# Four-layer graph network kernel: the one-hot matrices of the edge build get sixteen slots, four result buffers and a chunk-major stationary

## What is computed

```python
h = max(layernorm(x), 0); x = x + L0(h)   # sum of neighbours, two-layer MLP, layernorm
h = max(layernorm(x), 0); x = x + L1(h)   # 8-head attention over the edges, then an MLP
h = max(layernorm(x), 0); x = x + L2(h)   # softmax of the edge weights, both directions
h = max(layernorm(x), 0); x = x + L3(h)   # mean over neighbours, two linear maps
```

## Time and profile before

| | us |
|---|---|
| median of 3 runs (range) | 1474.82 (1468.77 to 1477.15) |
| the profiled execution | 1477.18 |
| its span, first to last instruction | 1475.4 |
| PE busy over the span | 1281.1 (87%) |
| DVE busy | 652.5 (44%) |
| ACT busy | 425.2 (29%) |
| set-up, to the first `hot` of DVE | about 49 |
| window stage, first matmul to first of line 424 | 50.05 to 365.04 |

### The profile page before, as it was taken

The page is one execution under the profiler, slowest core; times in us unless marked ns, Lnnn a source line. Parts: engine busy times, 40 slices in busy tenths (PEclk is TensorE's granted clock), DMA queues, the critical chain, the costliest instruction groups (busy, mean ns, idle before and its releaser), DMA issues.

```text
span 1475.4 us, 18831 instructions
## 1 busy us (share of the span) xinstructions
PE 1281.1 (87%) x6205; PEld 753.9 (51%) x6205; DVE 652.5 (44%) x1702; ACT 425.2 (29%) x728; POOL 126.7 (9%) x95
## 2 busy tenths in 40 slices
PE   1577777777999965998999999999998998899998
PEld 0244444444555432455777777775436555445543
DVE  6666666664401723103656565655565202430022
ACT  2401122222002422202555555553334202431000
POOL 0000000000445122100000000000233000100000
PEclk9878879778999987999999999999999999769999
DMA  4012344445777200000000000006000050000001
GB/s 131 0 34 58 99 136 124 137 123 143 280 262 267 86 0 28 30 28 1 1 2 1 1 1 1 2 2 233 1 0 30 0 202 1 1 29 0 0 29 41
DMA packets 41610, 93.86 MB, mean 64 GB/s; under 512 B 5113, under 2 KB 9920, under 8 KB 41526
## 3 DMA queue, kind: packets, MB, share of 16 engines
q1 hardware_dynamic: 41526, 92.74, 19.7%
HBM read 51.76 MB, written 34.56 MB: 59 GB/s over the span
## 4 chain that ended last, share of the span: by engine, by line
PE 78%; DVE 8%; issue 6%; ACT 4%; DVEq 2%; DMA 1%; SPq 0%; POOLq 0%; POOL 0%; ACTq 0%
PE PS L390 13%; PE PS L466 7%; PE PS L598 7%; PE PS L584 6%; PE PS L424 6%; PE PS L711 6%; PE PS L559 6%; PE PS L744 5%; PE PS L530 5%; PE PS L682 3%; PE PS L690 3%; PE PS L520 3%; PE PS L439 2%; DVE HT L865 2%; PE PS L463 2%
## 5 line engine op out<-in xcount | busy, mean ns | idle before, releaser
L390 PE MATMUL PS<-HT,R 125*128 (+1 forms) x988 | 243.3, 379 | 96.5 <-DVE HT L865 42.8
L865 DVE TENSOR_SCALAR HT<-BC,K 125x626 f16 (+1 forms) x494 | 193.0, 443 | 117.5 <-PE PS L390 71.6
L390 PEld LDWEIGHTS PS<-HT,R 125*128 x988 | 138.4, 158 | 201.4 <-issue 179.6
L960 DVE CUSTOM_DVE_ANT_0 HT<-PS,CD 128x1250 f32<-128x1250 f32 (+1 forms) x80 | 116.4, 1455 | 71.8 <-issue 71.8
L584 PE MATMUL PS<-K,HT 128*128 128x128 f32 (+2 forms) x800 | 120.4, 281 | 9.6 <-ACT R L1203 9.6
L1126 ACT COPY HT<-PS 128x626 f32<-128x626 f32 x80 | 54.6, 683 | 254.7 <-PE PS L390 254.7
L598 PE MATMUL PS<-R 128*64 128x128 f32 (+2 forms) x1600 | 113.0, 278 | 0.3
L1209 ACT ACTIVATE HT<-HT,soft 128x1250 f32<-128x1250 f32 (+1 forms) x80 | 106.3, 1333 | 11.7 <-DVE soft L963 11.6
L584 PEld LDWEIGHTS PS<-K,HT 128*128 128x128 f32 (+2 forms) x800 | 82.9, 140 | 43.7 <-issue 23.8
L559 PE MATMUL PS<-R 64*128 64x512 f32 (+3 forms) x480 | 96.5, 534 | 4.8 <-DVE soft L960 3.1
L1203 ACT COPY R<-PS 128x512 f32<-128x512 f32 (+1 forms) x120 | 65.2, 578 | 112.6 <-PE PS L584 112.6
(11 more groups left out here) (182 smaller groups left out, 1416.9 us busy)
## 6 DMA issues: line engine op xcount, KB each, us to landing
edge_parts<-HT SPq DMA_DIRECT2D x80, 234.4 KB
X<-edge_parts SPq DMA_DIRECT2D x15, 625.0 KB, 5.3
R<-edge_parts SPq DMA_DIRECT2D x15, 625.0 KB, 5.4
CD<-HT SPq DMA_DIRECT2D x160, 39.1 KB
edge_counts<-CD SPq DMA_DIRECT2D x10, 625.0 KB, 5.8
CD<-edge_sums SPq DMA_DIRECT2D x1, 6250.0 KB, 21.2
CD<-edge_counts SPq DMA_DIRECT2D x1, 6250.0 KB, 18.9
X<-in_x SPq DMA_DIRECT2D x2, 2304.0 KB
```

Source lines behind the costliest of these rows:

```text
L390: i = mm(bank(b0 + h, PIECE), stat, hot[:, h * PIECE:(h + 1) * PIECE], start=first, stop=True, skip_group_check=True)
L865: return ve.tensor_scalar(slot, iota[0:EC, :], K1[0:EC, K_BASE + w:K_BASE + w + 1], col, ALU.add, ALU.is_equal)
L960: ve.tensor_tensor_reduce(Pb[s][a][0:n], PS[0:n, a * N:(a + 1) * N], cd[0:n, t, :], 1.0, -3e38, ALU.add, ALU.max, soft[0:n, s, a:a + 1]).t ...
```

## The change

- `dst_oh` has the order (chunk, value): the 128 values of a chunk lie side by side, a chunk takes 128 elements. The same amount of `R0` is used. PE's stationary slices, the 32 comparisons, the three multiplications and POOL's zeroing are rewritten to this order; the comparisons now write elements that are 128 apart, and in the multiplications the weight part is repeated 32 times along the innermost dimension.
- The base slots of `src_oh` go from 2 x 3 to 4 x 3 (AHEAD = 4), so the slots are sixteen; DVE waits for window w - 4 in place of w - 2.
- `winbuf` has four buffers in place of three, and lies in `X` in place of `HT`, since the slots now fill `HT`. So ACT waits for its own ten tiles of `H` before the first copy, and each place that waits for all buffers has one semaphore more.

```diff
+AHEAD = 4
-WB_N = 3
+WB_N = 4
...
-        dst_oh = R0[:, :].bitcast(BF16).rearrange("p (m c) -> p m c", m=P)
-        src_oh = HT[0:EC, 0:(2 * FIX + TRIP * GEN) * HALFP // 2].bitcast(BF16)\
+        dst_oh = R0[:, :].bitcast(BF16).rearrange("p (c m) -> p c m", m=P)
+        src_oh = HT[0:EC, 0:(AHEAD * FIX + TRIP * GEN) * HALFP // 2].bitcast(BF16)\
...
-        winbuf = [HT[:, 3130 + q * HALFP:3130 + (q + 1) * HALFP] for q in range(WB_N)]
+        winbuf = [X[:, :, :].rearrange("p t o -> p (t o)")[:, q * HALFP:(q + 1) * HALFP] for q in range(WB_N)]
...
-            return w % 2 * FIX + q
+            return w % AHEAD * FIX + q
...
-            return bass.ds((n & (GEN - 1)) * TRIP + (2 * FIX + q), 1)
+            return bass.ds((n & (GEN - 1)) * TRIP + (AHEAD * FIX + q), 1)
...
-                    step(dst_oh[0:EC, :, bass.ds(lo, FIX)][:, :, q], src_oh[:, base_slot(w, q), :], q == 0)
+                    step(dst_oh[0:EC, bass.ds(lo, FIX), :][:, q, :], src_oh[:, base_slot(w, q), :], q == 0)
...
-                        i = step(dst_oh[0:EC, :, bass.ds(c, TRIP)][:, :, q],
+                        i = step(dst_oh[0:EC, bass.ds(c, TRIP), :][:, q, :],
...
-                i = ve.tensor_scalar(dst_oh[0:EC, j, 0:NC], low, float(j), None, ALU.is_equal)
+                i = ve.tensor_scalar(dst_oh[0:EC, 0:NC, j], low, float(j), None, ALU.is_equal)
...
-            shape = [EC, 2 * WIN, NC]
+            shape = [EC, NC, 2 * WIN]
             for q in range(3):
-                i = ve.tensor_tensor(dst_oh[0:EC, (q + 1) * 2 * WIN:(q + 2) * 2 * WIN, 0:NC],
-                                     dst_oh[0:EC, 0:2 * WIN, 0:NC],
-                                     wpart[q].unsqueeze(1).to_broadcast(shape), ALU.mult)
+                i = ve.tensor_tensor(dst_oh[0:EC, 0:NC, (q + 1) * 2 * WIN:(q + 2) * 2 * WIN],
+                                     dst_oh[0:EC, 0:NC, 0:2 * WIN],
+                                     wpart[q].unsqueeze(2).to_broadcast(shape), ALU.mult)
...
-                    if w >= 2:
-                        dve.wait_ge(sem("base_used"), FIX * (w - 2) + q + 1)
+                    if w >= AHEAD:
+                        dve.wait_ge(sem("base_used"), FIX * (w - AHEAD) + q + 1)
...
+            act.wait_ge(sem("l0_h"), T)
             for w in range(NW):
                 act.wait_ge(sem("base_used"), FIX * (w + 1))
...
-            gp.memset(dst_oh[0:EC, :, NC:NCP], 0.0).then_inc(sem("win_free"), PS_N)
+            gp.memset(dst_oh[0:EC, NC:NCP, :], 0.0).then_inc(sem("win_free"), PS_N)
```

More of the change, by code:

```diff
@@ L395, in base @@
                     pe.wait_ge(sem("base_oh"), FIX * w + q + 1)
-                    step(dst_oh[0:EC, :, bass.ds(lo, FIX)][:, :, q], src_oh[:, base_slot(w, q), :], q == 0)                        .then_inc(sem("base_used"), 1)
+                    step(dst_oh[0:EC, bass.ds(lo, FIX), :][:, q, :], src_oh[:, base_slot(w, q), :], q == 0)                        .then_inc(sem("base_used"), 1)
                 pe.wait_ge(sem("win_free"), w + 1)
```

## The result

The changed kernel takes **1505.15 us** in the median of four runs (1504.17 to 1507.98), the kernel before 1473.01 on the same chip (four runs, 1468.77 to 1477.15). The ratio is **1.0246, with a 95% interval of 1.0218 to 1.0275**: slower.

The account below looks back on a forecast made before the run. The window stage was taken as bound by PE's own instruction issue, with DVE's set-up chain adding directly. Products 16.0, comparisons 8.3 and slots -1 gave +23.3 us: 1500.5 profiled, 1498 at the median, range 1480 to 1511.

Parts of the forecast that it names:

- Products, +16.0: Set-up, line 823: three multiplications lose the double pace, 10.82 us each, 5.33 more each, 16.0 us in all.
- Comparisons, +8.3: Set-up, line 810: 32 comparisons slow from 235 to 493 ns each, the pace of line 816; +8.3 us.
- upper end of 18.9: Line 810: widely spaced writes add another 333 ns to each of the 32 comparisons; +18.9 us.
- the middle of three: Line 810: +8.3 us, chosen between +2.7 (output packing lost) and +18.9 (double cost for spaced writes).
- The rival in which spaced writes cost double: Set-up comparisons, line 810: +18.9 us in place of 8.3, total 1508 us; chance 0.10.
- Weight loads at nothing, with issue as the bound: Window stage: exposed load time, about 62 ns per matmul group, lies beside PE's sequencer work; 0 us gain counted.
- my two places: Signs of issue in the window stage: first-window rounds 1.42 us apart with 1.19 of matmuls; fifth-window 1.62 with 0.95 and 0.89.
- The rival of weight loads, 1485: Window stage: loads pace PE's groups, each of 207 gains up to 62 ns, 12.9 us; total 1485; chance 0.13.
- Table loads stay: Window stage: PE's table loads still at 0.9 us in the median from the ninth window on.
- The rival that spaced weight reads hold them up (1463): Window stage: side by side, PE's table loads fall to 0.54 us, 29.9 us off; total 1463; chance 0.08.
- Slots -1, buffers 0: Window stage: sixteen slots gain 1 us, between 0 and 6; four result buffers gain nothing, 13.3 us as other end.
- the rival at 1479: Window stage: late buffers caused PE's 13.3 us wait for ACT, comparisons +2.7; total 1479; chance 0.09, shared with unchanged product.

Follow-up runs that it names:

- The probe: Kernel before plus 18 set-up DVE instructions: comparisons at various spacings, products with real or repeated source; comparison 0.24 us packed, 0.88 at 8 apart; no kernel time given.
- cmp_one: Changed kernel with its 32 spaced comparisons put into one instruction writing value beside value; 1494.12 us, ratio 1.0177.

## Why the prediction was right, and where it wasn't

**The direction, the range and the place were right.** 1505.15 lies within 1480 to 1511, slower had 0.81, and the loss stands where the forecast put it, in the set-up's chain. 1498 was 7 us short.

**Products, +16.0: right.** 10.82 us forecast, 10821 ns measured. It was taken from the f32 slope, since one operand would no longer lie value beside value. The probe shows the reason by itself, and excludes the runs in the result.

**Comparisons, +8.3: the step that failed.** They cost 20.9 us, above even my upper end of 18.9. I took the middle of three, the pace at which nothing is packed, because no row of before had a spaced write. That is more than lost packing costs (at most 5.9 by cmp_one). But the write that goes to another 16 bytes each time is a cost of its own, 15 us or more here. The rival in which spaced writes cost double, at 1508, is what happened, and it had 0.10. Its pace of 0.826 us for one comparison (493 + 333 ns) is near the 0.80 measured from start to start; its 18.9 fell short because I took off the length of a record, 235 ns, and not the 153 ns between two starts, which gives +21.5. With 18.9 taken, the sum would have been +33.9 and the forecast near 1509, 4 us too high. The rule of the Trainium skill (VectorE: DVE Perf Modes, section on mode 2x_2P) that this mode asks for no unit step, by which the term was 2.7, agrees with the probe at 2 elements apart (0.35 us, near the 0.33 of f32) and gives too little from 4 on (0.52 and 0.88 us, lines 819 and 821).

**Weight loads at nothing, with issue as the bound: right.** The loads fell by 52 ns each, 51 us over 988, and the stage moved by 0.6. The matmul rounds are 1.59 us apart with 0.82 us of matmuls in them, and the sequencer's own instructions fill the rest. Nor did the layout help once part of the issue time was taken out, though landings held that stage. Of my two places, the first was no proof: in the first window 13 of the 18 rounds begin within 0.6 us of the end of DVE's pair, 0.39 at the least, and DVE in turn waits there for the round before last, so the two deep late slots hold PE too. Elsewhere this is so in 8 of 109 rounds, and the median over all is 2.3 us. The change left the late slots two rounds deep, so their part was not tried. I had said that a stage under 300 us would refute me; it stayed at 314.6. The rival of weight loads, 1485, is out: it needed a stage 13 us shorter.

**Table loads stay: right, for the reason given.** From the ninth window on the median is 796 ns, not 0.9 us, and over all 80 it fell from 876 to 778, but their sum by 1.3 us only. The rival that spaced weight reads hold them up (1463) is out, since taking the DMA traffic away shortens them beside those very reads.

**Slots -1, buffers 0: right in size.** Alone they gave 1.0027 (0.9994 to 1.006). The 13.3 us that PE seemed to wait for ACT are 13.4 with four buffers, so they were no late buffers; the rival at 1479 is out. Only with the table loads grouped did slots and fourth buffer together show, by 5.7 us of the stage in one pair of executions.

**The total.** My terms came to +23.3; measured at their places they are +37.3 (36.7 and 0.6), 14 us more. That the median came out only 32.1 above the one before is the remainder of the kernel, which no step of mine counted and which lies anywhere within 13 us. So part of this is luck: 1474.8 + 37.3 = 1512 lies just above my range, and that the time falls inside it, 7 us from my number, I owe to the remainder.

## What to carry to other kernels

Before a layout is turned for one reader, cost its writers: a 2-byte result written far apart costs DVE several times its packed pace (0.80 us against 0.15 for 320 here), and a repeated innermost source of a product nearly halves it. A shorter weight load is worth nothing where the sequencer between the matmuls sets the pace; look at the distance from round to round, not at the mean of a load. Registers fetched from SBUF inside such a loop are the first thing to group, above all beside heavy DMA traffic: here three lines of code were worth 1.6%, where the whole change cost 2.5%. What more buffers are worth can show only after that.

## What the runs showed of the hardware that was not expected

- A 2-byte comparison of 320 values: 0.24 us side by side, 0.35, 0.52 and 0.88 us at 2, 4 and 8 elements apart, flat to 62 (0.89). At 128, where the instructions overlap, 0.80 us from start to start. With two 2-byte sources: 0.32 side by side and 1.59 us at 62, 5.0 ns a result.
- A repeated second source alone nearly halves the pace of a 2-byte product (2.16 against 1.16 us for 1920); results or sources in runs of 32 change nothing (1.16).
- A table load took 296 ns for one register, 532 for two and 588 for eight, each at the least. Beside the stage's DMA traffic a load of two took up to 2.4 us.
- A weight load of 128 columns took 95 ns at the least with its values side by side and 143 with a step of 322. The Trainium skill (TensorE: Matmul & The Clock Gate, section on weight-path modes) names packed and strided reads alike for fast weight load; the rows show the strided one slower by half.
